# Attention and routed low-rank layer on one core: latent heads first, the two ordinary heads of a pair together, outputs stored over queries and keys

## The reference, cut to what matters

```python
x = hidden_states                                  # (1, 1024, 512)
q  = (x @ w_q) -> 32 heads of 128;  k, v = x @ w_k, x @ w_v -> 8 heads of 128
lk = ((x @ w_lq) @ w_lk) -> 32 heads of 128;       lv = (x @ w_lv) -> 32 heads of 128
q, k, lk = rope(q), rope(k), rope(lk);             k, v repeated 4 times
attn = causal_softmax(q @ k.T * scale) @ v         # "ordinary" heads, 4 share k and v
lat  = causal_softmax(q @ lk.T * scale) @ lv       # "latent" heads, same q
x = layernorm(x + attn @ w_o + lat @ w_lo)
x = layernorm(x + routed_lora(x))                  # top-1 of 8 experts, rank 16
```

## Time and profile before

| what | value |
|---|---|
| median of three runs | 2076.56 us (2076.46 to 2076.67) |
| the profiled execution, its own time | 2075.52 us |
| span of the profiled execution | 2073.7 us |
| mean granted clock of PE over the span | 0.994 |
| busy share PE, PEld, DVE, ACT, POOL | 97%, 88%, 68%, 50%, 51% |
| DMA | 50.86 MB in all, mean 25 GB/s |

### The profile page before, as it was taken

How to read it: one execution, slowest core, us unless ns; L and a number is a source line. 1 busy time by engine, 2 the same in 40 slices (tenths; PEclk the granted TensorE clock), 3 DMA queues, 4 the chain that set the end, 5 groups by cost and what they waited for, 6 DMA issues and landing times.

```text
span 2073.7 us, 39935 instructions
## 1 busy us (share of the span) xinstructions
PE 2010.6 (97%) x12832; PEld 1834.8 (88%) x12832; DVE 1405.2 (68%) x3404; ACT 1040.8 (50%) x2461; POOL 1059.7 (51%) x873
## 2 busy tenths in 40 slices
PE   6999999999999999999999999999999999999994
PEld 5988989899898989989899898998989899898993
DVE  5767757576675757757577675767767587575766
ACT  3654726355373644727356373654726456273651
POOL 5636465374654637545364554636455374653620
PEclk9999999999999999999999999999999999999998
DMA  5010010100001000010100001010010100100001
GB/s 172 2 34 11 2 55 1 44 1 32 25 1 44 2 32 24 1 44 1 55 1 17 28 1 55 1 34 11 2 55 1 34 11 22 35 1 31 2 11 41
DMA packets 19368, 50.86 MB, mean 25 GB/s; under 512 B 5825, under 2 KB 7873, under 8 KB 19009
## 3 DMA queue, kind: packets, MB, share of 16 engines
q1 hardware_dynamic: 19136, 48.00, 6.8%
HBM read 45.89 MB, written 2.10 MB: 23 GB/s over the span
## 4 chain that ended last, share of the span: by engine, by line
issue 46%; POOL 46%; PE 5%; DVE 1%; POOLq 1%; ACT 0%; DVEq 0%; ACTq 0%
POOL probs L673 26%; POOL probs L664 9%; POOL ql_lo L668 7%; POOL pt_lo L649 3%; PE ps L314 1%; PE ps L316 1%; PE ps L315 1%; POOLq L672 1%; POOL k_lo L668 1%; PE ps L401 1%; POOL wlk_lo L655 1%; DVE stats L805 0%; PE ps L496 0%; PE ps L511 0%; PE ps L488 0%
## 5 line engine op out<-in xcount | busy, mean ns | idle before, releaser
L673 POOL TENSOR_TENSOR probs<-probs,inv_sum 128x640 f32<-128x640 f32 (+7 forms) x512 | 586.0, 1147 | 491.9 <-DVE inv_sum L747 484.9
L680 DVE TENSOR_TENSOR pt_lo<-ps,pt_hi 128x512 fp32r<-128x512 f32 (+3 forms) x768 | 401.3, 550 | 202.0 <-ACT pt_hi L518 198.9
L550 ACT ACTIVATE probs<-probs,neg_max 128x640 f32<-128x640 f32 (+7 forms) x512 | 397.6, 777 | 163.6 <-DVE neg_max L740 163.6
L518 ACT ACTIVATE pt_hi<-ps 128x512 fp32r<-128x512 f32 (+3 forms) x768 | 347.0, 486 | 150.1 <-PE ps L401 137.1
L740 DVE CUSTOM_DVE_ANT_0 probs<-ps,mask 128x640 f32<-128x640 f32 (+7 forms) x512 | 382.6, 750 | 22.6 <-PE ps L401 19.4
L314 PE MATMUL ps<-pt_hi,val_hi 128*128 128x256 f32 (+1 forms) x1280 | 364.1, 284 | 14.5 <-DVE pt_lo L680 13.6
L315 PE MATMUL ps<-pt_lo,val_hi 128*128 128x256 f32 (+1 forms) x1280 | 360.5, 282 | 0.0
L316 PE MATMUL ps<-pt_hi,val_lo 128*128 128x256 f32 (+1 forms) x1280 | 359.8, 281 | 0.0
L401 PE MATMUL ps<-ident,probs 128*128 128x128 f32 x2304 | 336.4, 274 | 3.1 <-POOL probs L673 2.2
L401 PEld LDWEIGHTS ps<-ident,probs 128*128 128x128 f32 x2304 | 268.1, 140 | 29.6 <-DVE pt_lo L680 5.1
L649 POOL TENSOR_TENSOR pt_lo<-raw,pt_hi 128x1024 fp32r<-128x1024 f32 (+1 forms) x48 | 97.0, 2030 | 372.7 <-ACT pt_hi L518 372.7
(11 more groups left out here) (107 smaller groups left out, 4159.0 us busy)
## 6 DMA issues: line engine op xcount, KB each, us to landing
raw<-wo SPq DMA_DIRECT2D x32, 512.0 KB, 3.3
raw<-wq SPq DMA_DIRECT2D x16, 512.0 KB, 3.3
raw<-wlv SPq DMA_DIRECT2D x16, 512.0 KB, 3.9
raw<-wkv SPq DMA_DIRECT2D x8, 512.0 KB, 3.8
acc<-xT SPq DMA_DIRECT2D x4, 512.0 KB, 7.2
acc<-x SPq DMA_DIRECT2D x1, 2048.0 KB, 7.9
wlk_raw<-wlk SPq DMA_DIRECT2D x16, 128.0 KB, 3.9
out<-acc SPq DMA_DIRECT2D x8, 256.0 KB, 2.4
```

The lines of the kernel that those rows point to most:

```text
L518: return nc.scalar.activation(dst, src, ACT.Copy)
L550: nc.scalar.activation(dst, dst, ACT.Exp, bias=neg_max[:, n % 8:n % 8 + 1], scale=-1.0, accum_out=row_sum[:, n % 8:n % 8 + 1]).then_inc(q[ ...
L673: nc.gpsimd.tensor_tensor(b, b, inv_sum[:, k % 8:k % 8 + 1].to_broadcast([P, b.shape[-1]]), ALU.mult).then_inc(q["normed"], 1)
L680: return nc.vector.tensor_tensor(dst, src, h, ALU.subtract)
```

## The change

- **Order of the tiles** (`tile_of`). Tiles 0 to 15 are the latent ones of head 0 and then of head 1. Tiles 16 to 31 are the ordinary ones of both heads: query tile i of head 0 and of head 1 two tiles apart (4, 3, 4, 3, 5, 2, 5, 2, 6, 1, 6, 1, 7, 0, 7, 0).
- **Ordinary products.** The two heads have the same values, so one product takes query tile i of both: i + 1 blocks of 256 columns, none of 128. Latent products stay as they were.
- **Lags.** A tile is turned in slot n + 4 (was n + 3). Both kinds of products stand after the turning of their slot: long in slot n + 6, short in slot n + 7, which are both even slots.
- **Turned tiles.** `pt_hi`/`pt_lo` have three parts: long tiles take turns between two, short ones lie in the third at two places.
- **Outputs in place.** Latent results go over the latent keys as before, ordinary ones over the queries (`ql[:, 0:2]`); `o_hi`/`o_lo` are gone.
- **Output weights.** Two parts of 1024 columns, split after products 9 and 11, into `val_hi[:, 1:3]`/`val_lo[:, 1:3]`, the latent values, which are dead by then. ACT's wait for the output matmuls goes.
- **Output steps.** Latent steps first. Ten of the 32 steps (was three) stand ahead of the last products.
- **Units of pair 0.** The two k units move from behind the first q units to behind the latent keys.

```diff
-T_LAG = 3
+T_LAG = 4
-OUT_PARTS = (("ob", 0, 512, 1536), ("oa", 0, 1024, 0), ("ob", 512, 512, 1024))
-OUT_AFTER = (CHUNKS - 5, CHUNKS - 3, CHUNKS - 1)
+OUT_PARTS = ("oa", "ob")
+OUT_AFTER = (9, 11)
...
+HEADS_AT_ONCE = ((4, 3), (5, 2), (6, 1), (7, 0))
+def tile_of(n):
+    if n < 2 * ST:
+        return n // ST, 1, ORDER[n % ST]
+    return n % 4 // 2, 0, HEADS_AT_ONCE[n // 4 - ST // 2][n % 2]
...
-HEAD = {TILES - 2 + T_LAG: (0, 1, 2)}
+HEAD = {34: ((0, 0, 2),), 35: ((1, 0, 2), (2, 0, 2)), 36: ((0, 2, 4), (1, 2, 4))}
...
 def blocks_of_product(n):
-    return 2 * (ORDER[n % ST] // 2) + 2
+    a, latent, i = tile_of(n)
+    return 2 * (i // 2) + 2 if latent else i + 1
...
 for _n in range(2, TILES, 4):
-    _blocks = blocks_of_product(_n)
-    _k = _n + T_LAG + PV_LONG
-    PV_BEFORE[_k + 1] = (_n, 0, _blocks)
-    O_SLOT[_k + 2] = _n
+    PV_AFTER[_n + 6] = (_n, 0, blocks_of_product(_n))
+    O_SLOT[_n + 7] = _n
 for _n in range(3, TILES, 4):
-    _k = _n + T_LAG + PV_SHORT
-    PV_AFTER[_k] = (_n, 0, blocks_of_product(_n))
-    O_SLOT[_k + 1] = _n
+    PV_AFTER[_n + 7] = (_n, 0, blocks_of_product(_n))
+    O_SLOT[_n + 8] = _n
...
 def part_of_pt(n):
-    i = ORDER[n % ST]
-    return n % 2, 4 if i < 2 else 0, P * (i % 2)
+    a, latent, i = tile_of(n)
+    turn = n // 4 % 2
+    return 2 if n % 2 else turn, 4 * turn * (n % 2), P * (i % 2 if latent else a)
...
-        o_hi, o_lo = sb("o_hi", [P, 2, S], F32R), sb("o_lo", [P, 2, S], F32R)
-        pt_hi, pt_lo = sb("pt_hi", [P, 2, ST * 256], F32R), sb("pt_lo", [P, 2, ST * 256], F32R)
+        pt_hi, pt_lo = sb("pt_hi", [P, 3, ST * 256], F32R), sb("pt_lo", [P, 3, ST * 256], F32R)
...
+        wo_w = [w[:, 1:3].rearrange("p a t d -> p (a t d)") for w in (val_hi, val_lo)]
...
+        def output_part(n):
+            a, latent, i = tile_of(n)
+            if latent:
+                return [w[:, 2 + a, 256 * (i // 2):256 * (i // 2) + 256].rearrange("p (a n) -> p a n", n=P) for w in (ql_hi, ql_lo)]
+            return [w[:, 0:2, P * i:P * i + P] for w in (ql_hi, ql_lo)]
...
                 for j in range(j0, j1):
-                    q0 = P if j == last else 0
+                    q0 = P if latent and j == last else 0
...
                     if pair == 0:
                         weights_hi(g, "k")
-                    act.wait_ge(q["out_mm"], SEED + per_pair(g, pair, ST, 0))
                     if pair == 0:
                         weights_hi(g, "v")
```

More of the change, by code:

```diff
@@ L196, in parts @@
                 at, n = (0, 1024) if kind == "q" else (1024, 512)
-                return [w[:, 0, at:at + n].rearrange("p (c n) -> p c n", c=CT) for w in (pt_hi, pt_lo)]
+                return [w[:, 2, at:at + n].rearrange("p (c n) -> p c n", c=CT) for w in (pt_hi, pt_lo)]
             at, n = (0, HD) if kind == "v" else (HD, 2 * HD)
@@ L232, in output_weights, with output_step, product_of @@
         def output_weights(part, pair):
-            name, at, n, to = OUT_PARTS[part]
-            return (raw_of(f"{name}{pair}")[:, at:at + n], pt_hi[:, 1, to:to + n], pt_lo[:, 1, to:to + n])
+            return [raw_of(f"{OUT_PARTS[part]}{pair}")] + [w[:, 2 * D * part:2 * D * part + 2 * D] for w in wo_w]
+        def output_step(step):
+            latent, a = 1 - step // 2, step % 2
+            at = 2 * D * a + D * latent
+            return [w[:, 2 * latent + a, :] for w in (ql_hi, ql_lo)], [w[:, at:at + D] for w in wo_w]
+        def output_part(n):
[3 more added lines that the diff above has]
+            return [w[:, 0:2, P * i:P * i + P] for w in (ql_hi, ql_lo)]
+        def product_of(n):
+            m = chunk_after(n)
+            return ps[:, O_BANKS[m % len(O_BANKS)], 256 * (m % 2):256 * (m % 2) + 256].rearrange("p (a n) -> p a n", n=P)
         def raw_of(name):
@@ L259, in scores_of @@
         def scores_of(n):
-            banks, w = score_banks(n), P * (ORDER[n % ST] + 1)
+            banks, w = score_banks(n), P * (tile_of(n)[2] + 1)
             return ps[:, banks[0]:banks[-1] + 1, 0:w // len(banks)]
@@ L405, in with_values @@
             def with_values(g, pair, n, j0, j1):
-                m, step, c = chunk_after(n)
-                a, latent = divmod(step, 2)
-                last = 2 * c + 1
+                m = chunk_after(n)
+                a, latent, i = tile_of(n)
+                last = blocks_of_product(n) - 1
                 half, first, _ = part_of_pt(n)
@@ L424, in with_values, with outputs @@
                     mm.then_inc(q["pv_mm"], 1)
-            def outputs(g, pair, y, steps):
+            def outputs(g, pair, y, step0, step1):
                 t = OUT_ORDER[y]
-                if steps == (FIRST_STEP,):
-                    pe.wait_ge(q["maxed"], per_pair(g, pair, TILES, TILES - (y < 2)))
-                    pe.wait_ge(q["o_lo_made"], per_pair(g, pair, CHUNKS, (FIRST_STEP + 1) * ST // 2))
-                if steps[-1] == STEPS - 1:
-                    pe.wait_ge(q["o_lo_made"], per_pair(g, pair, CHUNKS, 3 * ST // 2 + y // 2 + 1))
-                if y >= 4:
-                    pe.wait_ge(q["out_added"], SEED + per_pair(g, pair, ST, y - 3))
-                for step in steps:
-                    a, latent = divmod(step, 2)
-                    lhs = [w[:, a, P * t:P * t + P] for w in ((ql_hi, ql_lo) if latent else (o_hi, o_lo))]
-                    made, at = STEP_WEIGHTS[step]
-                    if y == 0:
-                        pe.wait_ge(q["wo_lo"], SEED + per_pair(g, pair, len(OUT_PARTS), made))
-                    mm = three(ps[:, y % 4, :], lhs, [w[:, 1, at:at + D] for w in (pt_hi, pt_lo)],
-                               step == FIRST_STEP, step == STEPS - 1)
-                if steps[-1] == STEPS - 1:
+                if step0 == 0:
+                    if y < 3:
+                        pe.wait_ge(q["maxed"], per_pair(g, pair, TILES, TILES - (y < 2)))
+                    elif y == 3:
+                        pe.wait_ge(q["pt_lo_made"], per_pair(g, pair, T_UNITS, T_UNITS))
+                    else:
+                        pe.wait_ge(q["out_added"], SEED + per_pair(g, pair, ST, y - 3))
+                for step in range(step0, step1):
+                    if y == 0 and step < 2:
+                        pe.wait_ge(q["wo_lo"], SEED + per_pair(g, pair, len(OUT_PARTS), step + 1))
+                        pe.wait_ge(q["o_lo_made"], per_pair(g, pair, CHUNKS, ST // 2 * (step + 1)))
+                    if step == 2:
+                        pe.wait_ge(q["o_lo_made"], per_pair(g, pair, CHUNKS, ST + y + 1))
+                    out, weights = output_step(step)
+                    mm = three(ps[:, y % 4, :], [w[:, P * t:P * t + P] for w in out], weights, step == 0, step == STEPS - 1)
+                if step1 == STEPS:
                     mm.then_inc(q["out_mm"], 1)
@@ L462, in _ @@
                     for k in range(SLOTS):
-                        for y in HEAD.get(k, ()):
-                            outputs(g, pair, y, (FIRST_STEP,))
+                        for y, step0, step1 in HEAD.get(k, ()):
+                            outputs(g, pair, y, step0, step1)
                         if EARLY + MID <= k < TILES:
@@ L472, in _ @@
                             with_values(g, pair, *PV_AFTER[k])
-                    for steps in ((0, 1), (3,)):
-                        for y in range(2):
-                            outputs(g, pair, y, steps)
-                    outputs(g, pair, 2, (0, 1, 3))
-                    for y in range(HEADS, ST):
-                        outputs(g, pair, y, (2, 0, 1, 3))
+                    for y in range(ST):
+                        if BEGUN.get(y, 0) < STEPS:
+                            outputs(g, pair, y, BEGUN.get(y, 0), STEPS)
             ra = raw[:, 0, 0:CT * (E + E * R)].rearrange("p (c n) -> p c n", c=CT)
```

43 lines of the change are left out of this document (19 added, 24 removed), and 4 rows, old and new, of the table UNITS.

## The result

The change takes **2071.29 us** (median of 11 runs, 2070.00 to 2073.13) against 2076.46 before (11 runs, 2074.37 to 2076.93): ratio 0.9977, 95% interval 0.9968 to 0.9985. It is faster by 5.2 us where 33.8 were forecast, and lies 11 us above the range. The profiled execution has a span of 2070.8 us and a time of its own of 2072.64.

What follows compares the result with a forecast made beforehand. PE, busy 97% of the span, was taken to bound the kernel. Gains of 12.8 + 11.2 + 9.8 = 33.8 us from 2075.5 gave 2041.7, plus 1.0 for the median: 2042.7 us, range 2032.3 to 2060.

Steps and rivals of the forecast that it cites:

- Blocks of 128 columns: Ordinary products: 4 blocks of 256 columns replace 8 of 128, saving 0.80 us per pair, 12.8 us in all.
- Products after the shortest score tile: Five products per group each lose 0.28 us waiting; all taken as gone, 1.40 per group, 11.2 us.
- First product of a pair: At each pair's start the wait of about 1.1 us changes its releaser, not its size: 0, bounds 8 us either way.
- Pair ends: Waits in slots 31 and 35, 1.53 us per group, mostly go under output steps: gain 1.23 per group, 9.8 us.
- 0.65 if it misses like slot 31: Cost per pair if DVE misses emptying banks for tile 28's turning, as at pair 0's slot 31 before; 0.15 taken.
- the cover by the output steps: Four output steps between the last turning and tile 30's product give 1.4 us of cover for the 0.44 lost.
- Units, weights, queues: Earlier lv weights, pair 0's unit order and sooner loads cost PE nothing: 0; a mistake at most 6.8 us.
- rope wait: Pair 0's units, now k last, get no new wait for DVE's rope product; pair 1's 0.35 us wait stays.
- The waits only change place: Rival: DVE comes as late for PE's next bank, only the blocks count: 2063.7 us; chance 0.09.
- Slower: even slots too full: Rival: crowded even slots make PE wait 0.28 us per slot couple, up to 63 us: 2105.7 us; chance 0.05.
- PE's busy share (97%): Sign over the whole run: PE busy stays at 97% or above.
- the wait before tile 8: Sign: one wait of 0.7 to 1 us per pair before tile 8's scores, released by a DVE row maximum.

Runs made afterwards that it cites:

- both causes removed: The change with ACT's wait for the output matmuls restored and the output weights' low parts made by POOL instead of DVE: 2041.22 us, ratio 0.9829.
- the halves: On top of both causes removed, the last 256-column block of each ordinary product issued as two of 128: 2078.38 us.
- The experiment on 8 columns: The change with DVE's low parts of the output weights cut from 1024 to 8 columns, the rest left out: 2046.51 us, ratio 0.9853.
- the later loads: The change, ACT still without its wait, but SP's queue waits for the pair's last output product before loading output weights: 2065.54 us, ratio 0.9950.
- the wait put back: The change with ACT's wait for the output matmuls restored ahead of the v and lv weights: 2066.52 us, ratio 0.9951.

## Why the prediction was wrong, point by point

- **Blocks of 128 columns: right.** Their 12.8 us and the 11.2 of the next point make 3.0 us per group; measured, as the rest of the balance, 3.24 in the change, and 3.21 with both causes removed (249.55 - 245.06 = 4.49, of which 1.28 are in the listed waits). The balance does not part the two terms, but the price behind this one is borne out by the halves: 97 ns for a matmul that adds no column.
- **Products after the shortest score tile: right.** None of the products is listed with a wait any more, where 39 waits for `pt_lo` stood in the earlier trace rows.
- **First product of a pair: right.** 2.30 us per group before and after. It waits where it was said, before tile 8's scores, for DVE's maximum:

```profile
322.95 0.41 PE L334 MATMUL ps<-ql_hi 128*128 128x320 f32 x1 [0.57 <-DVE neg_max L752]
```

- **Pair ends: wrong, and this is most of it.** Two sentences failed: "ACT and DVE about 1 us each", and "I take 0.15 per pair, because on my count of DVE's operations the low parts of tile 26 end about when PE asks". The split takes 2.14 us on average, not 1, since it meets a POOL instruction; and it was counted only at the second of its two places. Forecast a gain of 1.23 per group, measured a loss of 1.21, and 0.66 more before the scores of tile 30, which no term held: (1.23 + 1.21 + 0.66) x 8 = 24.8 us short of the forecast. The experiment on 8 columns gives back 24.8 as well, though it measures something slightly different: the whole cost of the split (by group length 3.24 x 8 = 25.9), not the miss against the forecast. With the split off DVE the pair ends gain 1.73 - 0.33 = 1.40 per group, near the 1.23 forecast: the cover by the output steps was judged rightly, the price of the split was not. The bound ("0.65 if it misses like slot 31") was a third of the 1.80 per pair that it came to. The rows to see it were in the trace of before: there DVE split 512 columns in 0.69 us with POOL idle and in 1.00 with POOL at work, ending 0.55 us after POOL's instruction (127.77 + 0.61 = 128.38), each of 16 times. The rows of before, two of DVE and one of POOL:

```profile
127.93 1.00 DVE L680 TENSOR_TENSOR pt_lo<-raw,pt_hi 128x512 fp32r<-128x512 f32 x1
...
139.32 0.69 DVE L680 TENSOR_TENSOR pt_lo<-raw,pt_hi 128x512 fp32r<-128x512 f32 x1
```

```profile
127.77 0.61 POOL L673 TENSOR_TENSOR probs<-probs,inv_sum 128x256 f32<-128x256 f32 x1 [0.84 <-DVE inv_sum L747]
```

- **Units, weights, queues: wrong by one sentence.** "PE did not wait for them, as POOL had idle time, so this is 0", and the loads "start sooner, not later". Sooner was the harm: they moved onto the branch. 5.8 us by the later loads, 4.8 by the wait put back (7 boundaries of 0.78 are 5.5). The units cost 0.22 us per group more in the change, 1.8 us in all. Half of it is the restart right behind the boundary's gap and goes with that; the other half stays with both causes removed, and its cause was not looked for. No rope wait came there, as forecast.
- **The rivals and the signs.** "The waits only change place" was the nearest in time (2063.7) and had 0.09. But its mechanism, a DVE that is late everywhere, is not what happened: DVE is late where it is held. "Slower: even slots too full" did not come: its waits all along the even slots are missing, and none stands in the middle of a pair. Of the signs that the prediction named, PE's busy share (97%) and the wait before tile 8 came; the group got 0.37 us shorter and not 4.2.
- **The sum, corrected.** 33.8, less 24.8 for the pair ends, less 5.5 for the boundary, less 1.8 for the units, plus 1.9 on the first two terms, is 3.6. The profiled executions differ by 2.9 (2075.5 and 2072.64), the medians by 5.2.

## What to carry over

Price a moved instruction by what runs on the other engines at its new place, not by its own row: here the same subtraction is 1.23 or 2.1 us, and the engine that it moves off had time to spare. Where an engine that bounds the time has a loop, look at what the DMA queues do while it branches; a wait that seems useless may be what keeps the loads away. And when a gain is missing, restore the side edits one at a time: two side edits gave away 30 us that the main ones had earned.

## What the runs showed of the hardware

- A subtraction on DVE with both inputs in SBUF is held until the POOL instruction under way is over: 8 columns took 0.94 to 1.22 us, ending 0.02 us after POOL's; 1024 columns took 1.22 us alone and 2.00 to 2.28 beside POOL, ending 1.08 us after it. The profile shows the time of being held as busy, with no wait.
- TensorE's branch at the loop's end takes 3.33 us (median) with one packet of DMA beside it, and 4.55 with 0.82 MB (both from the window above). It ends 1.3 to 1.5 us after the one packet on the instruction queue, and the loads make that packet start at 1.85 to 2.43 us into the branch instead of 0.94 to 1.39. The Trainium skill's page "Runtime: NRT & Kernel Launch" (Instruction fetch mechanics) says that a taken branch outside the window forces a DMA fetch of its target before execution goes on. The trace agrees: one packet on the instruction queue beside each taken branch, none beside the one that leaves the loop (0.08 us), and the branch is late by as much as the packet.
- Halving a matmul of 256 columns into two of 128 costs 97 ns for each one more (384 more, 37.2 us).
